# The guard of the local streams' sums of squares, taken as the largest of pairs instead of a maximum with a constant

## The reference, cut to what matters

```
def l2norm(t):
    return t / jnp.clip(jnp.linalg.norm(t, axis=-1, keepdims=True), 1e-12)
...
q = l2norm(q) * qs
k = l2norm(k) * ksc
q, k = rotary_xpos(q, k)
o = local_attention(q, k, v)
```

## Time and profile before

| | |
|---|---|
| time, median of 3 runs | 3128.42 us (3126.73 to 3133.96) |
| profiled execution, its own time | 3130.85 us |
| its span, first to last instruction | 3128.7 us |
| PE busy | 2816.9 us, 90% of the span |
| DVE busy | 2411.2 us, 77% |
| ACT busy | 2147.9 us, 69% |
| POOL busy | 1548.2 us, 49% |
| mean granted clock of PE | 0.957 |

### The profile page before, as it was taken

One profiled execution on the slowest core, in us unless ns is written; L12 is line 12 of the kernel. 1 busy time (PEld: TensorE's weight loads), 2 busy tenths in 40 slices (PEclk: granted clock), 3 DMA queues, 4 the chain that ended last, 5 costly groups with the idle time before them and its releaser, 6 DMA issues.

```text
span 3128.7 us, 65895 instructions
## 1 busy us (share of the span) xinstructions
PE 2816.9 (90%) x22656; PEld 1976.8 (63%) x22656; DVE 2411.2 (77%) x6016; ACT 2147.9 (69%) x5956; POOL 1548.2 (49%) x1741
## 2 busy tenths in 40 slices
PE   3678999999999999999999999999999999998875
PEld 1455666666666666666666666666666666666553
DVE  3367888888888888888888888878888888777653
ACT  2356777777777777677777767777776777776653
POOL 1034554555545455554555554545555555545542
PEclk7689999999999999999999999999999999999987
DMA  2000000000000000000000000000000000000000
GB/s 67 3 3 4 5 6 6 5 6 6 6 5 7 6 4 6 6 6 6 5 7 6 5 6 6 6 5 7 6 5 6 6 6 5 6 4 4 4 5 5
DMA packets 41974, 21.76 MB, mean 7 GB/s; under 512 B 21131, under 2 KB 41013, under 8 KB 41653
## 3 DMA queue, kind: packets, MB, share of 16 engines
q1 hardware_dynamic: 41652, 17.55, 2.0%
HBM read 9.17 MB, written 4.19 MB: 4 GB/s over the span
## 4 chain that ended last, share of the span: by engine, by line
PE 43%; DVE 27%; ACT 19%; POOL 5%; issue 4%; DMA 0%; DVEq 0%; POOLq 0%; SPq 0%
DVE negmax L836 10%; ACT rawP L730 6%; ACT P L730 5%; PE bank L1050 5%; PE bank L1143 5%; PE bank L1151 4%; PE bank L1030 4%; PE bank L1096 3%; DVE ss L879 3%; PE bank L1159 3%; POOL rn L633 3%; PE bank L1130 2%; ACT probs L697 2%; PE bank L1085 2%; PE bank L1011 2%
## 5 line engine op out<-in xcount | busy, mean ns | idle before, releaser
L836 DVE TENSOR_REDUCE negmax<-bank 128x2 f32<-128x512 f32 (+1 forms) x896 | 554.4, 679 | 25.7 <-PE bank L1011 25.6
L697 ACT ACTIVATE probs<-bank 128x512 f32<-128x512 f32 (+1 forms) x1024 | 480.9, 568 | 131.8 <-PE bank L1030 129.5
L633 POOL TENSOR_TENSOR rn<-ss,minus_half 128x16 f32<-128x16 f32 x128 | 372.6, 2911 | 172.0 <-DVE ss L894 171.4
L582 POOL TENSOR_TENSOR veps<-moments,eps_tile 128x2 f32<-128x2 f32 x192 | 38.2, 199 | 785.4 <-DVE moments L788 785.4
L1085 PE MATMUL bank<-wqkv_sb,hS 128*128 128x512 f32 x768 | 390.9, 625 | 30.9 <-ACT P L730 12.7
L914 DVE TENSOR_REDUCE negmax<-bank 128x2 f32<-128x384 f32 (+1 forms) x384 | 211.7, 593 | 135.1 <-PE bank L1118 133.4
L600 POOL TENSOR_SCALAR_AFFINE_SELECT probs<-probs 128x256 f32<-128x256 f32 x512 | 225.2, 463 | 166.8 <-ACT probs L697 166.4
L1050 PE MATMUL bank<-probs,V 128*16 128x256 f32 (+1 forms) x4096 | 259.5, 373 | 24.4 <-ACT probs L697 22.2
L1011 PE MATMUL bank<-kT,qT 32*128 32x256 f32 (+1 forms) x2048 | 216.8, 324 | 25.7 <-DVE negmax L836 16.1
L1085 PEld LDWEIGHTS bank<-wqkv_sb,hS 128*128 128x128 f32 x768 | 131.9, 193 | 163.3 <-issue 125.6
L730 ACT ACTIVATE rawP<-bank,negmax 128x128 f32<-128x128 f32 x512 | 179.7, 376 | 79.7 <-DVE negmax L914 79.7
(11 more groups left out here) (138 smaller groups left out, 7299.2 us busy)
## 6 DMA issues: line engine op xcount, KB each, us to landing
xin<-x SPq DMA_DIRECT2D x32, 128.0 KB, 2.1
out<-xout SPq DMA_DIRECT2D x32, 128.0 KB, 1.8
V<-YB SPq DMA_DIRECT2D x64, 63.5 KB
wqkv_sb<-wqkv SPq DMA_DIRECT2D x1, 1536.0 KB
V<-YB SPq DMA_DIRECT2D x64, 0.2 KB
w_sb<-w SPq DMA_DIRECT2D x1, 682.0 KB
w_sb<-w SPq DMA_DIRECT2D x2, 256.0 KB
wo_sb<-wo SPq DMA_DIRECT2D x2, 256.0 KB
```

The source lines that it names most:

```text
L633: nc.gpsimd.tensor_tensor(rn[:, l, t].rearrange("p m h -> p (m h)"), ss[:, l, t].rearrange("p m h -> p (m h)"), minus_half[:], ALU.pow).th ...
L697: nc.scalar.activation(dst, src, ACT.Exp, scale=SCALE0 if k == ATTN0 else SCALE1)\
L836: nc.vector.reduce_max(negmax[:, k, t, head:head + 4 * many - 3:4], tile(u, e)[:, :].rearrange("p (h k) -> p h k", h=many), AX.X, negate=T ...
```

## The change

`ss` gets a last axis of two cells for each sum. Both are preset to 1e-24 by one more memset on POOL at the start (128 columns in all; `PRESETS` goes from 9 to 10). The sum of squares (L879) is written to cell 0 of each pair, so its 8 results are two elements apart; cell 1 keeps 1e-24. The guard becomes a reduction: the largest of each pair, 32 columns in, 16 out, written to a new tile `ss_kept`, which POOL's power then reads. The semaphores stay as they are.

```diff
-        ss = sb("ss", [P, 2, TT, 2, HEADS])
+        ss = sb("ss", [P, 2, TT, 2, HEADS, 2])
+        ss_kept = sb("ss_kept", [P, 2, TT, 2, HEADS])
...
-        PRESETS, CLEARED = 9, NBANKS
+        PRESETS, CLEARED = 10, NBANKS
...
+            nc.gpsimd.memset(ss[:], 1e-24).then_inc(setup_pool, 1)
...
-                    nc.gpsimd.tensor_tensor(rn[:, l, t].rearrange("p m h -> p (m h)"), ss[:, l, t].rearrange("p m h -> p (m h)"),
+                    nc.gpsimd.tensor_tensor(rn[:, l, t].rearrange("p m h -> p (m h)"), ss_kept[:, l, t].rearrange("p m h -> p (m h)"),
...
-                    nc.vector.reduce_sum(ss[:, l, t, m, :], squares[m][:, l], AX.X).then_inc(sig("sums", u), 1)
+                    nc.vector.reduce_sum(ss[:, l, t, m, :, 0], squares[m][:, l], AX.X).then_inc(sig("sums", u), 1)
...
-                    flat = ss[:, l, t].rearrange("p m h -> p (m h)")
...
-                    nc.vector.tensor_scalar(flat, flat, 1e-24, None, ALU.max).then_inc(sig("ss_ready", u), 1)
+                    nc.vector.reduce_max(ss_kept[:, l, t].rearrange("p m h -> p (m h)"), ss[:, l, t].rearrange("p m h e -> p (m h) e"), AX.X)\
+                        .then_inc(sig("ss_ready", u), 1)
```

## The result

The changed kernel takes 3096.41 us (median of 4 runs, 3091.66 to 3100.07), beside 3129.08 us for the kernel before (median of 4 runs, 3126.73 to 3133.96). The ratio is 0.9899, with a 95% interval of 0.9883 to 0.9914. The profiled execution took 3097.46 us, with a span of 3095.7.

A forecast was written before the change was run, and what follows sets the result against it. No engine bounds a whole round; undisturbed rounds take 89.62 us, plus clock falls. 3130.9 - 15.9 (stall) + 1.1 (guard) - 18 (clock) = 3098.1; that execution lies 2.4 over the median, so 3095.7 us, range 3085 to 3118.

The forecast's parts named there:

- The stall and what follows it: LOCAL0's half 0: the guard stops waiting for POOL, ACT's V copy is late next; 0.59 us a round, 15.9 us less.
- The new guard: DVE's reduction of 32 columns takes 181 ns, 20 more than now; two a round on the chain, 1.1 us more.
- Preset and pairs: POOL's extra memset at the start and DVE's sums written two elements apart: both zero; sums bounded by 1 us.
- The clock: Over the rounds: a shorter round breaks runs of clock falls; 18 us less, bounds 0 to 26.7.
- The wait did not move to L816: Rival: DVE's L816 waits for POOL instead, nothing is won; 3129.5 us; chance 0.07 for wait moved or absorbed.
- The slower one, by the clock: Rival: rounds only about 0.1 us shorter, falls repeat each round; 3168 us; chance 0.07, shared with a dearer guard.

The follow-up runs named there:

- the delay of 230 columns: Changed kernel plus one more DVE reduction, over 230 weight-tile columns, behind the guard of LOCAL0's half 0, result unread: 3096.90 us, ratio 0.9915.
- The delays: Changed kernel plus one unread DVE reduction behind the guard of LOCAL0's half 0; 230 columns: 3096.90 us; 930 columns: 3123.66 us.
- the kernels with 720 and 816 columns: Changed kernel plus one unread DVE reduction behind LOCAL0's half 0 guard; 720 columns: 3136.40 us, ratio 1.0046; 816: 3129.70 us, ratio 1.0027.

## Why the prediction was right, and where it was lucky

Predicted were 3095.7 us, within 3085 to 3118; measured were 3096.41.

**The stall and what follows it.** Right in place and size. Predicted: 0.56 to 0.63 us a round, 0.59 taken, less 0.04 for the dearer guards, 0.55. Measured: 0.56. The shift was to be 0.63 at L816 and is 0.62; 0.63 at POOL's addition and is 0.58, since the products took 0.04 us longer; 0.56 on PE and is 0.58. That the release of a 1.15 us stall is worth half of it, because ACT's copy of V comes next, is the step on which the whole estimate stood, and the delay of 230 columns shows it. One reading of the rows was not exact: the L884 at 1544.56 writes `rawQ`, and the 128 of that form reach 419 ns, not 417, which changes nothing in the argument.

**The new guard.** Predicted 181 ns, measured 173; 12 ns more than the old one's 161, not 20. The 181 came from reductions that read a bank. The delays, which read SBUF as the guard does, take 382 ns for 230 columns and 1112 for 930; a line drawn through these gives about 175 for 32. The kernel with the old guard in the three other places has rounds shorter by 0.05 us, where 2 x 0.012 = 0.02 us would be due; the rest is open.

**Preset and pairs.** As said: L879, now L881, keeps its 676 ns. The new memset takes 0.21 us at 9.18, and POOL's first work starts at 25.42 us instead of 25.41.

**The clock.** The sign was right, and the mechanism fits the traces: of the five slow rounds that followed directly on another slow one, none is left, and in the kernels with rounds of 89.0 to 89.1 us there are none or one, against one to five in those with 89.6. The size was lucky. I took 18 us; in the pair of profiles it is 15.9. But the kernel before gave 3122.51, 3121.78 and 3120.55 us as medians of 23, 19 and 14 runs on other chips, and the changed one 3100.05 and, with a hidden delay, 3096.90. There the gain is 22 to 26 us, so that 7 to 11 us remain for the clock. In hindsight my estimate rested on one execution's 26.7 us of losses, and a single execution's losses vary: the same program's runs span 26 us on one chip (3110.87 to 3136.75). The range held both outcomes; the likeliest value was right for the chip on which it was measured.

**The rivals.** The wait did not move to L816. The slower one, by the clock, did not come about for the reason given, that the gain was over 0.2 us a round; but the kernels with 720 and 816 columns show that a shorter round can be the slower one. They are shorter by 0.21 and 0.12 us in each undisturbed round than the kernel before, and slower by 0.46 and 0.27%. It was priced at 3168 us, which is too much: their medians are 3136 and 3130.

## What to carry to other kernels

Where a tiny DVE instruction takes over a microsecond at one place only, look at what POOL is doing at its start and end, and give the work a form that POOL doesn't hold up; here a reduction was one, and an operation with a second SBUF input was not. The changed kernel has more of such places: 59 of the 256 products at L904, which read two tiles from SBUF, take over 1.5 us where the shortest takes 0.67, and 28 of these lie on the chain that ended last. What they are worth was not tested. Value the cure by what comes late next, not by the length of the stall. And where the granted clock falls at a fixed place of a repeated round, a gain of one or two tenths of a microsecond a round can come out with the other sign: read the length of undisturbed rounds and count the slow ones before calling an edit good or bad.

## What the runs showed of the hardware that I had not expected

A maximum with a second tile from SBUF, 16 columns, is held up for as long as the one with a constant (1234 ns against 165), a way that the expectation had left open. And the falls of the clock can fall into step with the round. In all twelve traces every fall in the 26 rounds begins 37.7 to 41.0 us into its round. With an undisturbed round of 89.50 us and a slow one of 92.15 to 92.17, eight falls followed one another in eight rounds at the same place, 40.2 us in, at intervals of 92.16 us, as long as the 26 rounds were followed.
